# Graph attention on one core: edge steps of two slots and an accumulator that goes through TensorE and ScalarE

## The chip, the cores and the metric

One of the eight cores of a Trainium2 chip runs the whole program; the others are idle. The metric is device time in microseconds, from start to end of one execution. Engines are named as in the profile: PE is TensorE, DVE is VectorE, ACT is ScalarE, POOL is GpSimd, SP is SyncE, which here only issues DMAs.

## The reference

12,500 nodes with 256 features, 200,000 edges (src, dst), eight heads of 32. It is one attention layer over a graph with a residual and a layer norm:

```
q = (x @ Wq.T + bq) * 32**-0.5 ; k = x @ Wk.T + bk ; v = x @ Wv.T + bv    # per node, 8 heads
s = sum over a head of q[src] * k[dst]                                   # per edge and head
e = exp(s - max of s over the edges of the same src)
out = sum over the edges of e * v[dst] / sum of e                        # per src
y = layernorm(x + out @ Wo.T + bo)
```

## The kernel before

The program has three parts. `prepare` projects all nodes to q, k and v, writes a row [k | v and a one per head] of 520 floats per node to DRAM (`kv_rows`), sorts the edges by src, sorts the nodes by degree, and writes the q rows in that order (`q_perm`). `one_round` walks the edges; the diff touches only this part. `finish` divides, projects and normalises tile by tile.

A tile is 128 nodes of about the same degree, one per partition; there are 98 tiles. A tile's edges are walked in steps of G slots: in one step each partition handles G edges of its node. The number of steps of a tile is the largest degree in it, divided by G and rounded up. One round covers up to C edges of a node. STEPS is an upper bound that holds for any graph, fixed when the program is built: 598 before. The steps beyond the real ones work on a spare tile (number TILES) whose mask is NEG and whose columns are all 0, so all partitions gather row 0. A table `step_tab` holds tile and column of every step; each engine reads its entry into a register with `value_load`, which is a table load and some register operations on the engine's sequencer.

The accumulator `acc` lies in SBUF, VW = 264 columns per tile (eight heads of 32 sums and one weight sum). The softmax is computed online: `runmax` holds the maximum so far, and in each step the old accumulator is scaled by exp(old maximum − new maximum), which stands in `s` behind the G·8 scores.

All engines run their own loop over the same steps k, with B steps in a loop body, and meet on semaphores that count steps:

- GpSimd (`gather`, L931) issues G indirect DMAs per step, each 128 rows of 2080 bytes, into ring slot k mod U of `kv`. Before the last gather of a step it waits in `ready` (L923) for the indices, and for `pv_made` and `last_made` of the step that had the slot before.
- SyncE (`load_q`, L949 and L952) reads the tile number and loads q of the tile, into the ring `q`; it waits for `prod_made` of U steps ago.
- VectorE, in the order of `step`: sums of the products of k+1 (L797), weighting of the first V = G−1 slots of k (`weigh`, L825), look-up of step k+2 (L853, L854), copy of the old maximum (L802) and mask (L805) of k+1, new maximum of k+1 (L812), addition of the matmul sum of k−1 to the accumulator (`add_sum`, L844), product of k+2 (`score`, L790), scaling of the accumulator for k (`scale_acc`, L836), differences of k+1 (L818).
- ScalarE, per step: `indices` (L969 table load, L973) for the step U ahead, exp of k+1 (`weights`, L977), and the last slot's weighting, eight instructions of 33 columns, one per head (`weigh_last`, L987).
- TensorE (`total`, L1032 and L1034) multiplies an identity with the G weighted slots, so they add up in PSUM (`sum_ps`, two of them). A matmul of f32 shows as two records.

The waits on the semaphores are what sets the order between the engines; within an engine it is the order of the code.

## Time and profile before

| | us |
|---|---|
| median of 3 runs | 4026.59 |
| lowest, highest | 4025.29, 4100.18 |
| profiled execution | 4017.71 |
| its span in the profile | 4015.6 |
| VectorE busy | 3211.0 (80%) |
| GpSimd busy | 2447.6 (61%) |
| TensorE busy | 2227.2 (55%) |
| ScalarE busy | 1504.6 (37%) |

The share of a whole span mixes three stages. The edge loop is the stretch from about 1268 to 3723 us. Columns of the rows below are told with each view. "Idle before" of an engine is the time without work ahead of the instructions of a row, and what ended it; "issue" means that nothing which the profile shows was waited for. Sequencer work (waits, registers, branches, table loads) is not counted as busy; rows with a q behind the engine's name are of the sequencer. The clock PEclk is granted TensorE clock, 1 is full speed.

### The profile page before, as it was taken

To read this page: it belongs to the slowest core of one execution; us is meant where nothing else is said; L and a number is where in the kernel's file an instruction comes from. 1 tells how busy PE (TensorE), PEld (TensorE's weight loads), DVE (VectorE), ACT (ScalarE), POOL (GpSimd) and SP (SyncE) were. 2 spreads that over 40 slices of the span, in tenths; PEclk is the share of its full clock that TensorE was granted. 3 is DMA by queue.
4 is the path that set the end of the run, shared out by engine and by line. 5 is a ranking of instruction groups with operands and counts; after the bars stand their busy time and mean duration, and the time that the engine had idled before them with its cause. 6 is when DMAs were issued, how large, how long until landed. Compare 5 with 4: busy or idle time off the path is not lost. (4 is left out here: it accounts for less than half of the span.)

```text
span 4015.6 us, 59591 instructions
## 1 busy us (share of the span) xinstructions
PE 2227.2 (55%) x7109; PEld 1514.8 (38%) x7109; DVE 3211.0 (80%) x8164; ACT 1504.6 (37%) x6480; POOL 2447.6 (61%) x2365
## 2 busy tenths in 40 slices
PE   3999888653002555555555545555555555544776
PEld 3788775432001333333333333333333333323443
DVE  8554467799223999999999999999999999977776
ACT  0110002221001555555555555555555555534332
POOL 3221120003767777777777777777777777765677
PEclk9966568776555788778777787777877778766777
DMA  1211013226513788878887887888777788799222
GB/s 33 64 58 32 16 43 101 89 67 125 171 36 96 231 233 232 232 232 232 231 232 232 232 232 231 232 232 231 232 232 231 232 232 232 229 177 169 80 92 85
DMA packets 329217, 665.86 MB, mean 166 GB/s; under 512 B 63462, under 2 KB 191750, under 8 KB 329016
## 3 DMA queue, kind: packets, MB, share of 16 engines
q0 software_dynamic: 160768, 518.27, 46.4%
q1 hardware_dynamic: 168392, 146.96, 12.7%
q8 instruction: 20, 0.33, 0.0%
q14 instruction: 37, 0.30, 0.0%
HBM read 599.35 MB, written 65.86 MB: 166 GB/s over the span
## 5 line engine op out<-in xcount | busy, mean ns | idle before, releaser
L931 POOL DMA_INDIRECT kv<-kv_rows,idx x1794 | 1863.0, 1038 | 583.7 <-issue 538.5
L1032 PE MATMUL sum_ps<-pv,ident 128*128 128x264 f32 x2392 | 902.0, 512 | 1299.3 <-DVE pv L825 1299.3
L1032 PEld LDWEIGHTS sum_ps<-pv,ident 128*128 128x128 f32 x2392 | 511.3, 237 | 1712.1 <-DVE pv L825 1393.1
L987 ACT ACTIVATE pv<-kv,s 128x33 f32<-128x33 f32 x4784 | 1084.4, 309 | 53.9 <-ACT s L977 27.3
L790 DVE TENSOR_TENSOR prod<-kv,q 128x768 f32<-128x768 f32 x598 | 569.2, 952 | 59.7 <-DMA kv<-kv_rows,idx 59.6
L797 DVE TENSOR_REDUCE s<-prod 128x24 f32<-128x768 f32 x598 | 565.5, 946 | 0.0
L977 ACT ACTIVATE s<-s 128x32 f32<-128x32 f32 x598 | 137.0, 229 | 1126.1 <-DVE s L818 1126.1
L1034 PE MATMUL sum_ps<-pv,ident 128*128 128x264 f32 x1196 | 497.3, 508 | 0.0
L507 PE MATMUL hist_ps<-hot_lo,hot_hi 125*98 125x128 bf16 x1600 | 372.1, 409 | 121.7 <-DVE hot_hi L174 121.7
L825 DVE TENSOR_TENSOR pv<-kv,s 128x528 f32<-128x528 f32 x598 | 417.4, 698 | 0.3 <-ACT s L977 0.3
L507 PEld LDWEIGHTS hist_ps<-hot_lo,hot_hi 125*98 125x98 bf16 x1600 | 370.3, 259 | 123.2 <-issue 68.7
L492 POOL DMA_INDIRECT kv_st<-node_rows,node_id x98 | 102.8, 1049 | 464.4 <-issue 444.4
L472 POOL TENSOR_SCALAR hot_hi<-hi_b 125x320 bf16<-125x320 bf16 x140 | 149.7, 1072 | 377.8 <-PE hist_ps L507 356.7
L172 DVE TENSOR_SCALAR hot_lo<-lo_b 125x320 bf16<-125x320 bf16 x640 | 164.2, 334 | 206.5 <-PE hist_ps L507 206.5
L1034 PEld LDWEIGHTS sum_ps<-pv,ident 128*128 128x128 f32 x1196 | 296.6, 248 | 70.3 <-ACT pv L987 0.4
L844 DVE TENSOR_TENSOR acc<-acc,sum_ps 128x264 f32 x598 | 256.6, 429 | 22.2 <-PE sum_ps L1034 1.1
L575 ACT ACTIVATE kv_st<-kv_ps 128x256 f32<-128x256 f32 x98 | 37.6, 383 | 589.3 <-PE q_ps L519 589.3
L836 DVE TENSOR_TENSOR acc<-acc,s 128x264 f32 x598 | 255.0, 426 | 0.3
L518 PE MATMUL kv_ps<-w_sb,xt_sb 128*128 128x512 f32 x392 | 200.5, 636 | 0.0
L812 DVE TENSOR_REDUCE runmax<-s 128x32 f32 x598 | 123.7, 207 | 79.3
L973 ACT ACTIVATE idx<-cols 128x3 int32 x598 | 113.2, 189 | 139.0 <-DVE round_base L782 136.6
L1178 POOL DMA_INDIRECT x<-in_x_rows,node_id x98 | 112.7, 1150 | 56.9 <-issue 30.7
(164 smaller groups left out, 2450.5 us busy)
## 6 DMA issues: line engine op xcount, KB each, us to landing
q<-q_perm SPq DMA_DIRECT2D x598, 128.0 KB, 3.7
kv<-kv_rows,idx POOLq DMA_INDIRECT x1794, 4.0
kv_rows<-kv_st SPq DMA_DIRECT2D x98, 260.0 KB, 3.0
xt_sb<-in_xT SPq DMA_DIRECT2D x98, 128.0 KB, 3.2
node_rows<-q_st SPq DMA_DIRECT2D x98, 128.0 KB, 3.4
q_perm<-kv_st SPq DMA_DIRECT2D x98, 128.0 KB, 1.9
kv_st<-node_rows,node_id POOLq DMA_INDIRECT x98, 3.1
cols<-edge_keys,run_at POOLq DMA_INDIRECT x98, 2.5
```

The source lines that it names most:

```text
L172: dve.tensor_scalar(hot_lo[:, v, :], lo_b[:, c * CH:(c + 1) * CH], float(v), None, ALU.is_equal)
L507: last = pe.matmul(hist_ps[0:TILES, 0:P], hot_hi[:, :, e], hot_lo[:, :, e], start=c == 0 and e == 0, stop=c == CHUNKS - 1 and e == CH - 1)
L518: pe.matmul(ps[:, 0:b - a], xt_sb[:, j, kc, :], w_sb[:, kc, a:b], start=kc == 0, stop=False)
L790: dve.tensor_tensor(prod[:, :, :], kv[:, j, :, 0:D], q[:, j, :].unsqueeze(1).to_broadcast([P, G, D]), ALU.mult).then_inc(prod_made, 1)
L797: dve.tensor_reduce(s[:, b, 0:G * HEADS], prod[:, :, :].rearrange("p g (h d) -> p (g h) d", d=HD), AX.X, ALU.add).then_inc(scored, 1)
L825: dve.tensor_tensor(pv[:, b, 0:V * VW].rearrange("p (g h w) -> p g h w", g=V, w=HD + 1), kv[:, j, 0:V, D:KVW].rearrange("p g (h w) -> p g ...
L836: dve.tensor_tensor(at_tile, at_tile, s[:, b, G * HEADS:].unsqueeze(2).to_broadcast([P, HEADS, HD + 1]), ALU.mult).then_inc(acc_scaled, 1)
L844: dve.tensor_tensor(at_tile, at_tile, sum_ps[b][:, 0:VW], ALU.add).then_inc(acc_added, 1)
L931: pool.indirect_dma_start(out=kv[:, j, g, :], out_offset=None, in_=kv_rows, in_offset=bass.IndirectOffsetOnAxis(ap=idx[:, j, g:g + 1], axi ...
L987: last = act.activation(pv[:, b, V * VW + at_h:V * VW + at_h + HD + 1], kv[:, j, V, D + at_h:D + at_h + HD + 1], ACT.Copy, scale=s[:, b, V ...
L1032: pe.matmul(sum_ps[b][:, 0:VW], ident[:, :], pv[:, b, g * VW:(g + 1) * VW], start=g == 0, stop=False)
L1034: pe.matmul(sum_ps[b][:, 0:VW], ident[:, :], pv[:, b, V * VW:G * VW], start=False, stop=True).then_inc(summed, 1)
```

## The change

Steps have two slots (G = 2) and not three, a round has 40 columns per node and not 39, the rings have eight slots and not six, and loop bodies sixteen steps and not six. STEPS becomes 849. VectorE no longer reads and adds the matmul sum. Instead `carry` writes the scaled old accumulator into a third part of `pv`, TensorE adds it with a third matmul, and ScalarE copies the sum from PSUM to the accumulator (`store`), between the third and the fourth head of the next step; for that ScalarE reads the step's table entry a second time. `carry` of a step waits for the store of the step before. VectorE's look-up is cut in two: the table load right behind the sums of the products, the decoding behind the product. ScalarE makes its indices at the end of a step and not at the start. The scratch of the table building moves from `pv` to `kv`.

```diff
--- before.py
+++ after.py
@@ -36,14 +36,15 @@
 CHUNKS = EF // CH
 POOL_HOTS = 28
 CLIP = 1022
-G = 3
+G = 2
 QR = 2 * R
 BP = 65
-C = 39
+C = 40
 TAB = TILES + 1
-U = 6
+U = 8
 V = G - 1
-B = 6
+BEFORE_STORE = 3
+B = 16
 
 
 STEPS = C // G + (E // P + (TILES - 1) * (G - 1)) // G
@@ -695,11 +696,11 @@
         q = sb("q", [P, U, D])
         prod = sb("prod", [P, G, D])
         s = sb("s", [P, 2, (G + 1) * HEADS])
-        pv = sb("pv", [P, 2, G * VW])
...
@@ -797,9 +798,12 @@
                     dve.tensor_reduce(s[:, b, 0:G * HEADS], prod[:, :, :].rearrange("p g (h d) -> p (g h) d", d=HD),
                                       AX.X, ALU.add).then_inc(scored, 1)
 
-                def mask_scores(k, b, col, tile):
+                def old_maximum(k, b, tile):
 
                     dve.tensor_copy(s[:, b, G * HEADS:], runmax[:, bass.ds(tile * HEADS, HEADS)]).then_inc(old_copied, 1)
+
+                def mask_scores(k, b, col):
+
                     dve.wait_ge(scored, k + 1)
                     sv = s[:, b, 0:G * HEADS].rearrange("p (g h) -> p g h", h=HEADS)
                     dve.tensor_tensor(sv, sv, mflat[:, bass.ds(col, G)].unsqueeze(2).to_broadcast([P, G, HEADS]), ALU.add).then_inc(masked, 1)
@@ -827,58 +831,53 @@
                                       s[:, b, 0:V * HEADS].rearrange("p (g h) -> p g h", h=HEADS).unsqueeze(3).to_broadcast([P, V, HEADS, HD + 1]),
                                       ALU.mult).then_inc(pv_made, 1)
 
-                def scale_acc(k, b, tile, first=False):
-
+                def carry(k, b, tile, first=False):
                     if not first:
-                        dve.wait_ge(acc_added, k)
-                    dve.wait_ge(exp_made, k + 1)
-                    at_tile = acc[:, bass.ds(tile * VW, VW)].rearrange("p (h w) -> p h w", w=HD + 1)
-                    dve.tensor_tensor(at_tile, at_tile,
-                                      s[:, b, G * HEADS:].unsqueeze(2).to_broadcast([P, HEADS, HD + 1]), ALU.mult).then_inc(acc_scaled, 1)
-
-                def add_sum(k, b, tile):
-
-                    dve.wait_ge(acc_scaled, k + 1)
-                    dve.wait_ge(summed, k + 1)
-                    at_tile = acc[:, bass.ds(tile * VW, VW)]
-                    dve.tensor_tensor(at_tile, at_tile, sum_ps[b][:, 0:VW], ALU.add).then_inc(acc_added, 1)
+                        dve.wait_ge(acc_stored, k)
+                    dve.tensor_tensor(pv[:, b, G * VW:].rearrange("p (h w) -> p h w", w=HD + 1),
+                                      acc[:, bass.ds(tile * VW, VW)].rearrange("p (h w) -> p h w", w=HD + 1),
+                                      s[:, b, G * HEADS:].unsqueeze(2).to_broadcast([P, HEADS, HD + 1]), ALU.mult).then_inc(carry_made, 1)
 
                 dve.wait_ge(tab_ready, 1)
                 dve.wait_ge(runs_ready, 1)
 
-                tile_r = [dve.alloc_register(f"tile_{b}") for b in range(3)]
-                col_r = [dve.alloc_register(f"col_{b}") for b in range(3)]
-
-                def look_up(k, c):
-                    v = dve.value_load(step_tab[0:1, bass.ds(k, 1)], min_val=0, max_val=TAB * C * P - 1)
-                    dve.reg_mov(tile_r[c], v & (P - 1))
-                    dve.reg_mov(col_r[c], v >> PBITS)
+                tile_r = [dve.alloc_register(f"tile_{b}") for b in range(2)]
+                col_r = [dve.alloc_register(f"col_{b}") for b in range(2)]
+                entry_r = dve.alloc_register("entry")
+
+                def look_up(k):
+                    dve.reg_mov(entry_r, dve.value_load(step_tab[0:1, bass.ds(k, 1)], min_val=0, max_val=TAB * C * P - 1))
+
+                def decode(b):
+                    v = bounded(dve, entry_r, TAB * C * P - 1)
+                    dve.reg_mov(tile_r[b], v & (P - 1))
+                    dve.reg_mov(col_r[b], v >> PBITS)
 
                 def step(k, j, turn, peel=False, last=False):
 
                     b, b1 = j % 2, (j + 1) % 2
+                    tile, tile1, col1 = bounded(dve, tile_r[b], TILES), bounded(dve, tile_r[b1], TILES), bounded(dve, col_r[b1], TAB * C - G)
                     score_sum(k + 1, b1, peeled=peel and j == 0)
+                    look_up(k + 2)
+                    old_maximum(k + 1, b1, tile1)
                     weigh(k, j % U, b, peeled=peel and j < 2)
-
-                    tile, tile1, col1 = (bounded(dve, tile_r[j % 3], TILES), bounded(dve, tile_r[(j + 1) % 3], TILES),
-                                         bounded(dve, col_r[(j + 1) % 3], TAB * C - G))
-                    before = None if peel and j == 0 else bounded(dve, tile_r[(j + 2) % 3], TILES)
-                    look_up(k + 2, (j + 2) % 3)
-                    mask_scores(k + 1, b1, col1, tile1)
+                    mask_scores(k + 1, b1, col1)
+                    carry(k, b, tile, first=peel and j == 0)
                     maxima(k + 1, b1, tile1)
-                    if before is not None:
-                        add_sum(k - 1, b1, before)
                     if not last:
                         score(k + 2, (j + 2) % U, turn + (j + 2) // U)
-                    scale_acc(k, b, tile, first=peel and j == 0)
+                    decode(b)
                     differences(k + 1, b1, tile1)
 
-                look_up(0, 0)
-                look_up(1, 1)
+                look_up(0)
+                decode(0)
+                look_up(1)
+                decode(1)
                 score(0, 0, 0)
                 score_sum(0, 0, peeled=True)
                 tile, col = bounded(dve, tile_r[0], TILES), bounded(dve, col_r[0], TAB * C - G)
-                mask_scores(0, 0, col, tile)
+                old_maximum(0, 0, tile)
+                mask_scores(0, 0, col)
                 maxima(0, 0, tile)
                 score(1, 1, 0)
                 differences(0, 0, tile)
@@ -891,11 +890,8 @@
                     step(k, k - LOOPS * B, LOOPS * (B // U), last=k == STEPS - 2)
                 k = STEPS - 1
                 weigh(k, k % U, k % 2)
-                tile, before = bounded(dve, tile_r[k % 3], TILES), bounded(dve, tile_r[(k - 1) % 3], TILES)
-                add_sum(k - 1, (k - 1) % 2, before)
-                scale_acc(k, k % 2, tile)
-                add_sum(k, k % 2, tile)
-                for r in tile_r + col_r:
+                carry(k, k % 2, bounded(dve, tile_r[k % 2], TILES))
...
@@ -976,39 +972,54 @@
                     act.wait_ge(diffs_made, k + 1)
                     act.activation(s[:, b, :], s[:, b, :], ACT.Exp).then_inc(exp_made, 1)
 
-                def weigh_last(k, j, turn, b, peeled=False):
+                def weigh_heads(j, b, heads):
+
+                    for h in heads:
+                        at_h = h * (HD + 1)
+                        last = act.activation(pv[:, b, V * VW + at_h:V * VW + at_h + HD + 1], kv[:, j, V, D + at_h:D + at_h + HD + 1],
+                                              ACT.Copy, scale=s[:, b, V * HEADS + h:V * HEADS + h + 1])
+                    return last
+
+                def weigh_last(k, j, turn, b, stored=True, peeled=False):
 
                     act.wait_ge(exp_made, k + 1)
                     act.wait_ge(kv_in[j], 16 * G * turn + 16 * G)
                     if not peeled:
                         act.wait_ge(summed, k - 1)
-                    for h in range(HEADS):
-                        at_h = h * (HD + 1)
-                        last = act.activation(pv[:, b, V * VW + at_h:V * VW + at_h + HD + 1], kv[:, j, V, D + at_h:D + at_h + HD + 1],
-                                              ACT.Copy, scale=s[:, b, V * HEADS + h:V * HEADS + h + 1])
-                    last.then_inc(last_made, 1)
+                    weigh_heads(j, b, range(0, BEFORE_STORE))
+                    if stored:
+                        store(k - 1, 1 - b)
+                    weigh_heads(j, b, range(BEFORE_STORE, HEADS)).then_inc(last_made, 1)
+
+                def store(k, b):
+
+                    v = act.value_load(step_tab[0:1, bass.ds(k, 1)], min_val=0, max_val=TAB * C * P - 1)
+                    tile = bounded(act, v & (P - 1), TILES)
+                    act.wait_ge(summed, k + 1)
+                    act.activation(acc[:, bass.ds(tile * VW, VW)], sum_ps[b][:, 0:VW], ACT.Copy).then_inc(acc_stored, 1)
 
                 act.wait_ge(tab_ready, 1)
                 act.wait_ge(runs_ready, 1)
                 for j in range(U):
                     indices(j, j, 0)
                 weights(0, 0)
-                weigh_last(0, 0, 0, 0, peeled=True)
+                weigh_last(0, 0, 0, 0, stored=False, peeled=True)
                 for k in range(B):
-                    indices(k + U, k % U, 1)
                     weights(k + 1, (k + 1) % 2)
                     weigh_last(k + 1, (k + 1) % U, (k + 1) // U, (k + 1) % 2, peeled=k == 0)
+                    indices(k + U, k % U, 1)
                 with act.Fori(1, LOOPS - 1) as kk:
                     for j in range(B):
                         k = kk * B + j
-                        indices(k + U, j % U, kk * (B // U) + j // U + 1)
                         weights(k + 1, (j + 1) % 2)
                         weigh_last(k + 1, (j + 1) % U, kk * (B // U) + (j + 1) // U, (j + 1) % 2)
+                        indices(k + U, j % U, kk * (B // U) + j // U + 1)
                 for k in range((LOOPS - 1) * B, STEPS - 1):
+                    weights(k + 1, (k + 1) % 2)
+                    weigh_last(k + 1, (k + 1) % U, (k + 1) // U, (k + 1) % 2)
                     if k + U < STEPS:
                         indices(k + U, k % U, (k + U) // U)
-                    weights(k + 1, (k + 1) % 2)
-                    weigh_last(k + 1, (k + 1) % U, (k + 1) // U, (k + 1) % 2)
+                store(STEPS - 1, (STEPS - 1) % 2)
 
             @block.tensor
             def _(pe):
@@ -1023,19 +1034,17 @@
                     last = pe.matmul(tab_ps[2 * j + 1][:, 0:b - a], nsteps[0:TILES, :], past[0:TILES, a:b], start=True, stop=True)
                 last.then_inc(counts_made, 1)
 
-                def total(k, b, peeled=False):
+                def total(k, b):
 
                     pe.wait_ge(pv_made, k + 1)
-                    if not peeled:
-                        pe.wait_ge(acc_added, k - 1)
                     for g in range(V):
                         pe.matmul(sum_ps[b][:, 0:VW], ident[:, :], pv[:, b, g * VW:(g + 1) * VW], start=g == 0, stop=False)
                     pe.wait_ge(last_made, k + 1)
-                    pe.matmul(sum_ps[b][:, 0:VW], ident[:, :], pv[:, b, V * VW:G * VW], start=False, stop=True).then_inc(summed, 1)
-
-                for j in range(B):
-                    total(j, j % 2, peeled=j < 2)
-                with pe.Fori(1, LOOPS) as kk:
+                    pe.matmul(sum_ps[b][:, 0:VW], ident[:, :], pv[:, b, V * VW:G * VW], start=False, stop=False)
+                    pe.wait_ge(carry_made, k + 1)
+                    pe.matmul(sum_ps[b][:, 0:VW], ident[:, :], pv[:, b, G * VW:], start=False, stop=True).then_inc(summed, 1)
+
+                with pe.Fori(0, LOOPS) as kk:
                     for j in range(B):
                         total(kk * B + j, j % 2)
                 for k in range(LOOPS * B, STEPS):
```

## Rows read from the trace of the kernel before

**Rows 1.** source view of L790: count, duration ns min/median/max, first and last start

```profile
L790 DVE TENSOR_TENSOR prod<-kv,q x598: 949/951/992, 1267.8 to 3715.3; 128x768 f32<-128x768 f32 x200
```

**Rows 2.** groups of 1500 to 3300 us: busy, mean ns | idle before

```profile
L931 POOL DMA_INDIRECT kv<-kv_rows,idx x1347 | 1390.1, 1032 | 410.7 <-issue 410.7
L987 ACT ACTIVATE pv<-kv,s 128x33 f32<-128x33 f32 x3590 | 813.8, 309 | 41.1 <-ACT s L977 21.0 <-PE sum_ps L1034 4.4
...
L790 DVE TENSOR_TENSOR prod<-kv,q 128x768 f32<-128x768 f32 x449 | 427.1, 951 | 0.0
```

**Rows 3.** windows: stretch, us, busy per engine, PEclk, DMA share, GB/s

```profile
2000.00:2500.00 500.00, 264.68 (x750) 166.01 (x750) 467.94 (x1124) 266.17 (x1246) 385.99 (x375) 0.79 0.80 232
...
3557.00:3703.00 146.00, 71.19 (x164) 43.91 (x163) 104.01 (x244) 57.60 (x269) 91.10 (x82) 0.65 0.98 177
3760.00:3990.00 230.00, 169.43 (x566) 105.87 (x567) 183.93 (x730) 76.12 (x122) 179.11 (x162) 0.74 0.29 92
```

**Rows 4.** timeline, one step: start us, duration us, instruction

```profile
2508.26 0.95 DVE L797 TENSOR_REDUCE s<-prod 128x24 f32<-128x768 f32 x1
2508.38 0.23 ACT L977 ACTIVATE s<-s 128x32 f32<-128x32 f32 x1 [1.91 <-DVE s L818]
2508.79 1.82 ACT L987 ACTIVATE pv<-kv,s 128x33 f32<-128x33 f32 x8 [0.17 <-PE sum_ps L1034]
...
2509.13 0.70 DVE L825 TENSOR_TENSOR pv<-kv,s 128x528 f32<-128x528 f32 x1
...
2509.88 1.16 PE L1032 MATMUL sum_ps<-pv,ident 128*128 128x264 f32 x4 [1.12 <-DVE pv L825]
2509.89 0.17 DVE L802 COPY s<-runmax 128x8 f32 x1
2510.03 0.18 DVE L805 TENSOR_TENSOR s<-s,mask 128x24 f32<-128x24 f32 x1
2510.35 0.21 DVE L812 TENSOR_REDUCE runmax<-s 128x32 f32 x1
...
2510.57 0.43 DVE L844 TENSOR_TENSOR acc<-acc,sum_ps 128x264 f32 x1
...
2510.92 0.95 DVE L790 TENSOR_TENSOR prod<-kv,q 128x768 f32<-128x768 f32 x1
...
2511.79 0.43 DVE L836 TENSOR_TENSOR acc<-acc,s 128x264 f32 x1
2512.13 0.19 DVE L818 TENSOR_TENSOR s<-s,runmax 128x32 f32<-128x32 f32 x1
...
2512.35 0.23 ACT L977 ACTIVATE s<-s 128x32 f32<-128x32 f32 x1 [1.65 <-DVE s L818]
```

**Rows 5.** source view of L949, SyncE's first table load

```profile
L949 SPq TENSOR_LOAD <-tile_tab x598: 262/268/290, 1137.2 to 3683.6; - x200
```

**Rows 6.** timeline of ScalarE reading PSUM in the first part

```profile
149.54 0.38 ACT L575 ACTIVATE kv_st<-kv_ps 128x256 f32<-128x256 f32 x1
149.82 0.38 ACT L576 ACTIVATE kv_st<-kv_ps 128x256 f32<-128x256 f32 x1
```

**Rows 7.** source view of L969, ScalarE's table load

```profile
L969 ACTq TENSOR_LOAD <-step_tab x598: 272/278/303, 1259.8 to 3694.1; - x200
```

**Rows 8.** timeline, TensorE at the lower clock

```profile
2501.70 2.13 PE L1032 MATMUL sum_ps<-pv,ident 128*128 128x264 f32 x4 [2.29 <-DVE pv L825]
```

**Rows 9.** windows over rows 8 and over the step of rows 4

```profile
2499.20:2509.30 10.10, 6.22 (x13) 3.70 (x12) 9.43 (x23) 5.02 (x24) 7.66 (x9) 0.50 0.80 233
2509.60:2522.90 13.30, 5.88 (x23) 4.12 (x24) 12.40 (x33) 7.51 (x36) 10.25 (x11) 1.00 0.81 231
```

**Rows 10.** DMA queues from 3557 to 3703 us: packets, MB, share

```profile
q0 software_dynamic: 6714, 22.34, 87.2%
```

**Rows 11.** page, DMA queue that carries code: packets, MB, share

```profile
q8 instruction: 20, 0.33, 0.0%
```

**Rows 12.** page, DMA issues: count, us from issue to landing

```profile
kv<-kv_rows,idx POOLq DMA_INDIRECT x1794, 4.0
```

More of the change, by code:

```diff
@@ L697, in one_round @@
         s = sb("s", [P, 2, (G + 1) * HEADS])
-        pv = sb("pv", [P, 2, G * VW])
-        room = pv[:, :, :].rearrange("p b w -> p (b w)")
-        step_f, past, tile_f = room[:, 0:STEPS], room[:, STEPS:2 * STEPS], kv[0:1, U - 1, :, :].rearrange("p g w -> p (g w)")[:, 0:STEPS]
-        place_f = prod[0:1, :, :].rearrange("p g d -> p (g d)")[:, 0:STEPS]
+        pv = sb("pv", [P, 2, (G + 1) * VW])
+        room = kv[:, :, :, :].rearrange("p u g w -> p (u g w)")
+        step_f, past = room[:, 0:STEPS], room[:, STEPS:2 * STEPS]
+        tile_f, place_f = room[0:1, 2 * STEPS:3 * STEPS], room[0:1, 3 * STEPS:4 * STEPS]
         tab_ps = [pp("tab_ps0", [1, 512]), pp("tab_ps1", [1, 512]), pp("tab_ps2", [1, 512]), pp("tab_ps3", [1, 512])]
@@ L713, in one_round @@
             sem(x) for x in ("prod_made", "scored", "old_copied", "masked", "max_made", "diffs_made"))
-        exp_made, pv_made, last_made, acc_scaled, summed, acc_added = (
-            sem(x) for x in ("exp_made", "pv_made", "last_made", "acc_scaled", "summed", "acc_added"))
+        exp_made, pv_made, last_made, carry_made, summed, acc_stored = (
+            sem(x) for x in ("exp_made", "pv_made", "last_made", "carry_made", "summed", "acc_stored"))
         CUT = 512
@@ L893, in _ @@
                 weigh(k, k % U, k % 2)
-                tile, before = bounded(dve, tile_r[k % 3], TILES), bounded(dve, tile_r[(k - 1) % 3], TILES)
-                add_sum(k - 1, (k - 1) % 2, before)
-                scale_acc(k, k % 2, tile)
-                add_sum(k, k % 2, tile)
-                for r in tile_r + col_r:
+                carry(k, k % 2, bounded(dve, tile_r[k % 2], TILES))
+                for r in tile_r + col_r + [entry_r]:
                     dve.free_register(r)
```

## The prediction, made before the change was run

> **What bounds the kernel now.** I read the busy time by stage first, then the groups of the steady stretch, then one step in order of time, then the same step on TensorE at its two clocks, and last the stretch at the end of the edge loop.
>
> The edge loop runs from the first product at 1267.8 us to the last at 3715.3 us, 598 steps [rows 1]. That is 2447.5 of the 4015.6 us span; only this part changes. In the steady part a step takes 1800/449 = 4.01 us: VectorE starts 449 products in 1800 us and none of them waits for data [rows 2]. VectorE is busy for 468 of 500 us [rows 3], and its nine instructions follow one another with hardly a gap [rows 4]. So VectorE sets the step.
>
> Second in line is GpSimd. It starts a gather every (1390.1+410.7)/1347 = 1.337 us [rows 2], three a step, which is also 4.01 us: no room above VectorE. This number becomes the floor when VectorE gets shorter. TensorE and ScalarE have slack inside a step today, because nothing that they make is needed at once: the sum of step k is added one step later.
>
> The last idle steps are another regime. Between 3557 and 3703 us there are 82/3 = 27.3 steps, so 5.34 us each, with the DMA engines at 0.98 of their time [rows 3]. These are the steps beyond the real work: all partitions gather the same row.
>
> **How many steps.** The nodes are sorted by degree and a tile needs ceil(largest degree / G) steps. From the reference's inputs (98 tiles, largest degrees 32 down to 7) that is 559 real steps of 598 with three slots, and 813 of 849 with two. Check on the trace: 559 × 4.01 + 39 × 5.34 = 2450 us, against 2447.5. After the change 813 steps are to be paid with a shorter step, and 36 idle ones. Gathers fall from 1794 to 1698. To break even, (2450 − 133)/813 = 2.85 us a step is allowed (the 133 is the idle part, below).
>
> **VectorE's step after.** By row: the product of 768 columns takes 0.95, the 264 column ones 0.43, so 1.03 ns a column [rows 4]. From start to start: sum of products 0.87 − 256 × 1.03 ns = 0.60; copy of the old maximum about 0.12; weighting of one slot 0.34 (as L836 to L818); mask 0.15; carry 0.34; maximum 0.2 (as L812 to L844); product 0.87 − 0.26 = 0.61; difference 0.10. Sum 2.46 us. The addition of 0.35 is gone (L844 to L790), and the wait between mask and maximum (L805 to L812, 0.32) is filled by the carry. The look-up is sequencer work of under a microsecond; its halves lie behind the 0.60 and the 0.61 and cost 0 to 0.1, I take 0. The loop's end comes 51 times and not 98; a gain of at most a few tens of us if VectorE set the step, which it won't; I take 0. Alone, VectorE would allow 813 × 2.46 = 2000 us.
>
> **GpSimd's step after.** 2 × 1.337 = 2.67 us. It has now less than before to wait for, and a ring of eight buffers. SyncE loads q 849 times instead of 598; it waits on a product eight steps back, so only its traffic counts: 2 gathers and one q in about 2.8 us is no more per us than 3 gathers and one q in 4.01. The larger table is built well before the loop: SyncE reads its first entry at 1137.2 us, 130 us before the first product [rows 5]. Both cost nothing.
>
> **What the accumulator's new way costs.** This is the step on which the forecast rests. ScalarE now does, per step: exp, three heads, the store of the previous sum, five heads, indices. The heads are handed on 0.216 us apart ((1.82 − 0.31)/7, [rows 2, 4]). The store reads PSUM like L575: 0.38 long, and the next one starts 0.28 after it [rows 6]. ScalarE alone: 0.41 to the first head + 3 × 0.216 + 0.28 + 5 × 0.216 + 0.10 + exp to exp 0.1 = 2.6 us. That is no bound by itself. But the accumulator makes two rings that close once per step.
>
> Ring 1, through VectorE. The store of k sits between the heads of k+1; carry(k+1) waits for it, and behind carry on VectorE are queued the maximum, the product and the difference of k+2, for which the next exp waits. From the start of exp to the start of the store: 0.41 from exp to the first head [rows 4] and three heads give 1.05; beside them the new table read, 0.28 [rows 7] and the register operations around it, may end sooner or later: 0.9 to 1.2 for the whole. Then the store 0.38, carry 0.34, maximum 0.2, product 0.61, difference 0.19, and three hand-overs of 0.03. Sum 2.7 to 3.0, I take 2.80.
>
> Ring 2, through TensorE. After the store come five heads (0.28 + 4 × 0.216 + 0.31 = 1.45), then TensorE's last slot and the carry, one behind the other, then the next store. Two such matmuls from a standing start, four records, take 1.16 us at full clock and 2.13 us at half clock [rows 4, 8]; 0.05 + 0.04 for the hand-overs (L825 ends 2509.83, TensorE starts 2509.88, [rows 4]). Sum 2.70 at full clock, 3.67 at half clock. carry_made is earlier than last_made and is not late; the late one is always last_made.
>
> Today the half clock costs nothing: six records, 1.5 times the 2.13, are about 3.1 of 4.01 us and nobody waits. After the change its price is on the path. The granted clock has two levels, 1.2 and 2.4 GHz: one stretch stands at 0.50 and the next at 1.00 [rows 9]. Its mean is 0.79 in the loop, so full for 0.58 of the time, 0.65 in the idle steps, and 0.74 in the stage after the loop [rows 3]. Its share after the change is not shown; bounds are 0.30 full (the idle steps) and 1 (the stretch at 1.00). After the change TensorE is busy about as in the last stage, so I take 0.53, between 0.48 there and 0.58 now. Steps per us: 0.53/2.80 + 0.47/3.67 = 0.317, so 3.15 us a step.
>
> **The sum.** Real steps 813 × 3.15 = 2561. Idle steps: of 5.34 us the gathers' queue has 0.872 [rows 10], 4.66 or 1.55 a gather, the rest 0.6; two gathers give 3.7, times 36 is 133. Together 2694 against 2450: +244. The profiled execution has 4017.7 us, 2 us of them outside its span; that makes 4262. The median shown is 4026.6, 9 us higher; I say 4265.
>
> **Rivals.**
>
> A, faster. The rings close sooner and GpSimd sets the step: 813 × 2.67 + 133 = 2304, −146, 3870. For it: the ScalarE work is 2.6, both rings at full clock begin at 2.70, and a TensorE that is at full clock nearly always would leave the step at GpSimd's pace. It decides below 2.75 us a step, which is 2% faster. Against it: every one of three terms must fall at its low end. Chance 0.21.
>
> B, the rings hold but TensorE keeps the full clock: 813 × 2.80 + 133 = 2409, −41, 3977. For it: at full clock six records take about 1.7 us (1.5 times 1.16), now of 4.01 and then of 2.8. Against it: in the last stage TensorE is busy 169/230 = 74% of the time and in the loop 53%, and yet the mean clock is lower there [rows 3]. The Trainium skill (TensorE: Matmul & The Clock Gate, Part 1: The HAM clock gate) says that the default is the throttled clock and that being busy releases it; by that rule the change raises the share of full clock and the time would be this one. The trace agrees only from the idle steps to the loop (0.65 to 0.79), not on to the last stage. Chance 0.17, up to 2.95 us a step.
>
> C, slower still: the longer loop body costs a code load in each of the 51 passes. In the trace there are 20 code transfers of 0.33 MB in all on the one queue [rows 11], fewer than the 98 passes, so today the loop runs without them. What one would cost is not shown: nothing at the least, and at the most what a transfer from HBM takes from issue to landing, 4.0 us for a gather [rows 12]. With 3 us it is +150, 4415. The Trainium skill (Runtime: NRT & Kernel Launch, Instruction fetch mechanics) says that code is held in two blocks of 256 instructions and that a jump back to a block that is no longer there stalls; by my count of the listing (about 25 VectorE instructions a step) sixteen steps are some 400 instructions, which may lie in three blocks, where six steps were about 155. The trace before can't show it. Chance 0.11.
>
> D: the change does nothing measurable in this loop, 4027. It would need the step to fall by exactly the rise in steps; chance 0.02, taken with B.
>
> **How the numbers follow.** Forecast 0.49: its own range comes from the share of full clock, 0.75 (2.98 us, 4120) to 0.45 (3.22 us, 4320). The range 3870 to 4400 reaches from A to just under C; what is left out is about half of A and most of C with the end of the forecast's own. 2% of 4027 is 81 us, about what a measurement can tell from no change. Faster 0.21 (A), within 2% 0.18 (B, D and a little of the forecast), slower 0.61.
>
> **What would show it.** Right: in the steady part VectorE waits before the carry for the store (ScalarE) in most steps, ScalarE waits before the store for TensorE's sum where the granted clock is 0.50 and hardly where it is 1.00; step lengths in two kinds, near 2.8 and near 3.7; GpSimd now waits for last_made. Idle steps of 3.7. Wrong: VectorE waiting at the product for gathers and GpSimd without a gap, which is A; a granted clock near 1 throughout, which is B; one long gap per sixteen steps on VectorE or ScalarE together with some fifty code transfers, which is C. VectorE's own instructions adding up to much more than 2.46 would break the working at its first term.

## The result and the profile after

The changed kernel takes 4292.2 us (median of 4, 4290.1 to 4296.2) against 4035.7 us of the kernel before in the same runs: ratio 1.065, 95% interval 1.061 to 1.068. One of the four runs of the kernel before, 4100.2 us, was in a slower state of the chip and is left out of the ratio. The forecast was 4265 us, in a range of 3870 to 4400. The profiled execution has a span of 4289.5 us, 274 more than before. All but 2 us of it is in the edge loop. First the source view of the product (duration min/median/max, first and last start), then the windows of the steady part and of the idle steps (busy time per engine, granted clock, DMA share, GB/s):

```profile
L791 DVE TENSOR_TENSOR prod<-kv,q x849: 672/681/755, 1269.4 to 3989.0; 128x512 f32<-128x512 f32 x170
```

```profile
1500.00:3500.00 2000.00, 1272.88 (x3760) 689.99 (x3758) 1553.37 (x5011) 1572.67 (x6890) 1279.35 (x1253) 0.90 0.75 209
3870.00:3980.00 110.00, 68.19 (x176) 36.23 (x175) 73.28 (x234) 72.80 (x321) 61.49 (x58) 0.77 0.92 176
```

The loop has 849 products in 2719.6 us, where it had 598 in 2447.5 [rows 1]: +272. VectorE's share fell from 94% to 78% of a steady stretch [rows 3], GpSimd's from 77% to 64%, ScalarE's rose from 53% to 79%. No engine is full any more; what sets the step is a ring of waits: a chain that starts at one instruction and comes back to the same instruction one step later. The granted clock rose from 0.79 to 0.90.

The steps are of three kinds: the plain step, the one with a code load (place 1), and those at half clock behind it. From start to start of the product, by place in the pass of 16 steps (medians over the 813 real steps, us; a pass is one run through the loop body):

```
place   0     1     2     3     4 to 8   9     10 to 13   14    15
       2.85  5.97  3.79  3.83   2.86    3.04     2.86    3.00  2.78
```

The plain step, in order of time (start, duration; TensorE at full clock):

```profile
2019.72 0.39 ACT L999 ACTIVATE acc<-sum_ps 128x264 f32 x1
...
2020.01 1.16 ACT L979 ACTIVATE pv<-kv,s 128x33 f32<-128x33 f32 x5
...
2020.26 0.43 DVE L837 TENSOR_TENSOR pv<-acc,s 128x264 f32<-128x264 f32 x1 [0.22 <-ACT acc L999]
...
2020.70 0.68 DVE L791 TENSOR_TENSOR prod<-kv,q 128x512 f32<-128x512 f32 x1
...
2021.22 0.71 PE L1043 MATMUL sum_ps<-pv,ident 128*128 128x264 f32 x2 [0.49 <-ACT pv L979]
2021.30 0.18 DVE L822 TENSOR_TENSOR s<-s,runmax 128x24 f32<-128x24 f32 x1
...
2021.51 0.22 ACT L973 ACTIVATE s<-s 128x24 f32<-128x24 f32 x1 [0.25 <-DVE s L822]
...
2021.77 0.75 ACT L979 ACTIVATE pv<-kv,s 128x33 f32<-128x33 f32 x3
2021.77 0.61 PE L1045 MATMUL sum_ps<-pv,ident 128*128 128x264 f32 x2
...
2022.58 0.39 ACT L999 ACTIVATE acc<-sum_ps 128x264 f32 x1
```

Both rings can be walked here. Store 2019.72 to 2020.11, carry 2020.26 (VectorE idle for 0.22 before it, ended by the store), maximum, product, difference until 2021.48, exp, three heads, store 2022.58: ring 1. Five heads until 2021.17, last slot 2021.22, carry behind it until 2022.38, store 2022.58: ring 2. 2.86 us from store to store.

One step in sixteen and those behind it (same columns):

```profile
2187.36 0.69 DVE L798 TENSOR_REDUCE s<-prod 128x16 f32<-128x512 f32 x1 [3.02 <-ACT pv L979]
...
2188.91 1.25 PE L1041 MATMUL sum_ps<-pv,ident 128*128 128x264 f32 x2 [3.66 <-DVE pv L829]
...
2192.11 0.39 ACT L999 ACTIVATE acc<-sum_ps 128x264 f32 x1 [0.82 <-PE sum_ps L1045]
...
2192.66 0.43 DVE L837 TENSOR_TENSOR pv<-acc,s 128x264 f32<-128x264 f32 x1 [1.14 <-ACT acc L999]
...
2193.62 1.25 PE L1043 MATMUL sum_ps<-pv,ident 128*128 128x264 f32 x2 [0.82 <-ACT pv L979]
...
2194.66 1.09 PE L1045 MATMUL sum_ps<-pv,ident 128*128 128x264 f32 x2
...
2195.94 0.39 ACT L999 ACTIVATE acc<-sum_ps 128x264 f32 x1 [1.04 <-PE sum_ps L1045]
```

The sum of products at 2187.36 comes after 3.02 us of idle VectorE. The view puts this down to ScalarE's heads, but the wait in front of the sum is for the heads of three steps earlier, which had ended some 6 us before. It is VectorE's sequencer that stands: it jumps back to the start of the body at 2183.84 and shows nothing until 2187.05 (L886). ScalarE's sequencer stands as well, from its jump at 2186.54 to 2190.04 (L1011); that is hidden behind VectorE's delay, because the difference for which ScalarE's next exp waits ends only at 2190.08.

TensorE has nothing to do for 3.66 us in this time, and from 2188.91 on it runs at half clock. In the second step behind the load its last slot and carry take from 2193.62 to 2195.75, 2.13 us, and the store at 2195.94 waits 1.04 us for them; the carry at 2192.66 had waited 1.14 us for its store, which had itself waited for TensorE. Such a step is 3.8 us. On the page one queue shows what the 3 us are (packets, MB; first the kernel before, then the changed one):

```profile
q14 instruction: 37, 0.30, 0.0%
```

```profile
q14 instruction: 547, 4.48, 0.3%
```

The row that I had put forward, [rows 11], was the other code queue, which has hardly changed (21 transfers). 510 more of 8 KB in 51 passes is ten a pass. The waits of 1500 to 3500 us (total, times, longest) in short: the carry waits for the store in 548 of 627 steps, the store for TensorE's sum in 83. The sum of products stands 35 times but up to 3.6 us; these are the code loads, under ScalarE's name.

```profile
DVE pv L837 <- ACT acc L999: 197.9, 548, 1.2
DVE s L798 <- ACT pv L979: 112.4, 35, 3.6
ACT acc L999 <- PE sum_ps L1045: 77.5, 83, 1.0
```

The account of the 813 real steps, from the means by place (50.8 passes): 813 × 2.856 = 2322 us of plain steps; the code load 3.02 × 50.8 = 153; the steps at half clock behind it 2.04 × 50.8 = 104; the other places that are longer or shorter than the plain step 13. Sum 2592, or 3.19 a step.

### The profile page after: what moved, and what is told of

The parts are those of the page before. It is cut to its first block and busy times, and to the rows that moved or that the text cites. A ratio compares the mean times of both kernels' runs of the same rounds, so it can differ in the third digit from the quotient of the medians.

```text
span 4289.5 us, 77637 instructions
## 1 busy us (share of the span) xinstructions
PE 2663.5 (62%) x8615; PEld 1641.2 (38%) x8615; DVE 3069.9 (72%) x9574; ACT 2358.0 (55%) x9839; POOL 2330.8 (54%) x2269
## 5 line engine op out<-in xcount | busy, mean ns | idle before, releaser
L979 ACT ACTIVATE pv<-kv,s 128x33 f32<-128x33 f32 x6792 | 1621.4, 312 | 48.5 <-ACT s L973 25.8
L1041 PE MATMUL sum_ps<-pv,ident 128*128 128x264 f32 x1698 | 676.5, 484 | 701.8 <-DVE pv L829 701.8
L1043 PE MATMUL sum_ps<-pv,ident 128*128 128x264 f32 x1698 | 660.5, 474 | 423.7 <-ACT pv L979 423.3
L798 DVE TENSOR_REDUCE s<-prod 128x16 f32<-128x512 f32 x849 | 582.2, 686 | 177.1 <-ACT pv L979 141.6
L791 DVE TENSOR_TENSOR prod<-kv,q 128x512 f32<-128x512 f32 x849 | 579.1, 682 | 21.7 <-DMA kv<-kv_rows,idx 21.5
L1045 PE MATMUL sum_ps<-pv,ident 128*128 128x264 f32 x1698 | 575.3, 424 | 0.0
L837 DVE TENSOR_TENSOR pv<-acc,s 128x264 f32<-128x264 f32 x849 | 367.2, 433 | 276.9 <-ACT acc L999 270.4
L999 ACT ACTIVATE acc<-sum_ps 128x264 f32 x849 | 331.2, 390 | 149.4 <-PE sum_ps L1045 107.7
L973 ACT ACTIVATE s<-s 128x24 f32<-128x24 f32 x849 | 189.0, 223 | 400.1 <-DVE s L822 400.1
L829 DVE TENSOR_TENSOR pv<-kv,s 128x264 f32<-128x264 f32 x849 | 367.7, 433 | 1.2 <-ACT s L973 0.3
L803 DVE COPY s<-runmax 128x8 f32 x849 | 149.8, 176 | 144.8 <-issue 142.4
L969 ACT ACTIVATE idx<-cols 128x2 int32 x849 | 161.7, 191 | 139.8 <-DVE round_base L783 136.5
```

The costliest lines, as they stand in the source:

```text
L791: dve.tensor_tensor(prod[:, :, :], kv[:, j, :, 0:D], q[:, j, :].unsqueeze(1).to_broadcast([P, G, D]), ALU.mult).then_inc(prod_made, 1)
L798: dve.tensor_reduce(s[:, b, 0:G * HEADS], prod[:, :, :].rearrange("p g (h d) -> p (g h) d", d=HD), AX.X, ALU.add).then_inc(scored, 1)
L829: dve.tensor_tensor(pv[:, b, 0:V * VW].rearrange("p (g h w) -> p g h w", g=V, w=HD + 1), kv[:, j, 0:V, D:KVW].rearrange("p g (h w) -> p g ...
L837: dve.tensor_tensor(pv[:, b, G * VW:].rearrange("p (h w) -> p h w", w=HD + 1), acc[:, bass.ds(tile * VW, VW)].rearrange("p (h w) -> p h w" ...
L973: act.activation(s[:, b, :], s[:, b, :], ACT.Exp).then_inc(exp_made, 1)
L979: last = act.activation(pv[:, b, V * VW + at_h:V * VW + at_h + HD + 1], kv[:, j, V, D + at_h:D + at_h + HD + 1], ACT.Copy, scale=s[:, b, V ...
```

## The experiments

Ratios are to the kernel before, timed beside each run; "before" is 4017 to 4042 us in these. Theory 1: two rings, and a code load in each pass that also costs TensorE its clock. The steps by place are read from each run's starts of the product.

**Shorter body.**

```diff
-B = 16
+B = 8
```

> The changed kernel with loop bodies of 8 steps instead of 16; nothing else. Theory 1 (two separate causes: a code load of about 3.1 us on VectorE and ScalarE in each pass of the 16-step loop, and behind it, because TensorE stood idle, some three steps at half clock of 3.8 instead of 2.86 us): with 187 VectorE instructions a pass no code is loaded, the clock stays full, a step is 2.87 us, the loop 813 x 2.87 + 36 x 3.64 = 2464 us, the whole 4035 us, about the kernel before. Rival H (the half clock comes by itself, as it did before the change, and the code loads only add to it): the loads go (-158) but one step in six stays at 3.8 us: 4130 us. Rival N (the long step in each pass is the loop's own end, not code): no fewer long steps per step, rather more: 4290 us or above.

Measured: 4061.5 us, ratio 1.009 (1.006 to 1.012), 231 less than the change as it stands. Code transfers and the window from 1500 to 3400 us:

```profile
q14 instruction: 41, 0.34, 0.0%
```

```profile
1500.00:3400.00 1900.00, 1219.89 (x3914) 635.49 (x3912) 1618.14 (x5219) 1639.26 (x7175) 1494.98 (x1305) 1.00 0.79 228
```

The transfers are gone and the granted clock is 1.00 throughout: the half clock did not come by itself, it followed the stall. H and N fall. The plain step stays at 2.86; two steps of every eight, right behind the jump, take 3.04 and 3.12. For them above all, the real steps took 37 us more than expected; the idle steps took 9 less.

**TensorE's order, in the 16-step body.**

```diff
-                    pe.wait_ge(last_made, k + 1)
-                    pe.matmul(sum_ps[b][:, 0:VW], ident[:, :], pv[:, b, V * VW:G * VW], start=False, stop=False)
                     pe.wait_ge(carry_made, k + 1)
-                    pe.matmul(sum_ps[b][:, 0:VW], ident[:, :], pv[:, b, G * VW:], start=False, stop=True).then_inc(summed, 1)
+                    pe.matmul(sum_ps[b][:, 0:VW], ident[:, :], pv[:, b, G * VW:], start=False, stop=False)
+                    pe.wait_ge(last_made, k + 1)
+                    pe.matmul(sum_ps[b][:, 0:VW], ident[:, :], pv[:, b, V * VW:G * VW], start=False, stop=True).then_inc(summed, 1)
```

> The changed kernel, with 16-step bodies, but TensorE takes the carry before the last slot: behind last_made there is then one matmul and not two. Theory 1 (ring 2 through TensorE sets the steps at half clock and only those; ring 1 through VectorE sets the others): steps at half clock fall from 3.8 to about 2.9 us, steps at full clock stay at 2.86, code loads stay: 51 x 2.9 x 0.9 = 133 us less, 4160 us. Rival (the steps of 3.8 us are ScalarE or VectorE catching up after the code load): no change, 4290. Rival (ring 2 sets the full-clock steps too): these shorten as well, by up to 0.4 us, below 4050.

Measured: 4199.1 us, ratio 1.042 (1.037 to 1.047), 93 less. Places 3 and 4 of the pass fall from 3.52 and 3.24 (means) to 2.95 and 2.88. The step right behind the load (place 2) keeps its 3.79 us:

```profile
2159.80 1.25 PE L1041 MATMUL sum_ps<-pv,ident 128*128 128x264 f32 x2 [4.65 <-DVE pv L829]
...
2160.20 0.69 DVE L791 TENSOR_TENSOR prod<-kv,q 128x512 f32<-128x512 f32 x1
...
2161.72 1.09 PE L1045 MATMUL sum_ps<-pv,ident 128*128 128x264 f32 x2
...
2163.01 0.39 ACT L999 ACTIVATE acc<-sum_ps 128x264 f32 x1 [0.84 <-PE sum_ps L1045]
...
2163.99 0.68 DVE L791 TENSOR_TENSOR prod<-kv,q 128x512 f32<-128x512 f32 x1
```

Here all that TensorE needs has been made, and its six records run back to back, 3.01 us at half clock; their order can't matter. So ring 2 sets the later steps at half clock and TensorE's whole work the first one. The gain is made up otherwise than I expected: of 83 us in the real steps, places 2 to 6 give 58, and 28 come from steps at full clock, of which some (places 0 and 10 to 13) fall from 2.86 to 2.77. To that small part the second rival was right; why those places and no others is open.

**Carry behind the product, and both together,** in the 8-step body:

```diff
-                    carry(k, b, tile, first=peel and j == 0)
                     maxima(k + 1, b1, tile1)
                     if not last:
                         score(k + 2, (j + 2) % U, turn + (j + 2) // U)
+                    carry(k, b, tile, first=peel and j == 0)
                     decode(b)
```

Both versions also make the copy of the old maximum wait for the carry of two steps before, which reads the same part of `s`. "Both" has TensorE's new order as well.

> The changed kernel with 8-step bodies and the carry behind the next product on VectorE instead of ahead of the maximum. Theory 1 (ring 1, store - carry - maximum - product - difference - exp - heads - store, sets the 2.86 us): 0.8 us leave this ring, the next bound is ring 2 at full clock or GpSimd, 2.70 us: 813 x 2.72 + 131, 3920 us. Rival (ScalarE's own work and its second table load set 2.86): no change against 8-step bodies alone, 4035. Rival (the carry is now late for TensorE): 0.3 us more a step, 4250.

> 8-step bodies, carry behind the product, and TensorE takes the carry before the last slot. Theory 1: both rings are below GpSimd's two gathers (2.67 us a step), which then sets the step: 813 x 2.68 + 131, 3885 us, and VectorE waits at the product for gathers. Rival (ScalarE, 2.6 us of work and the hand-overs, is the bound): 2.75 to 2.8 us a step, 3960. Rival (carry ahead of the last slot makes TensorE wait for the late carry): slower than the version with the carry late alone.

Measured: late alone 4066.8 us, 1.011 (1.008 to 1.013), as with B = 8 alone; both 4103.3 us, 1.018 (1.013 to 1.023). Theory 1 missed both times. In the second TensorE waits 1.1 us for the late carry in every step, its last slot queued behind it (total us, times, longest, 1500 to 3400 us):

```profile
PEld sum_ps L1045 <- DVE pv L839: 697.4, 640, 1.2
```

which is the rival that both texts named. That late alone gains nothing fits the next three runs: ring 2 was still closed. It was not tested further.

**One ring at a time, without touching VectorE's order.** b8_swap is B = 8 with TensorE's new order; b8_early is B = 8 with ScalarE's table load ahead of the exp:

```diff
+                        tile = tile_of(k)
                         weights(k + 1, (j + 1) % 2)
-                        weigh_last(k + 1, (j + 1) % U, kk * (B // U) + (j + 1) // U, (j + 1) % 2)
+                        weigh_last(k + 1, (j + 1) % U, kk * (B // U) + (j + 1) // U, (j + 1) % 2, tile)
```

This is the part in the loop's body; `tile_of` is the table load that `store` had in it.

> 8-step bodies (step 2.86 us at full clock, whole 4061 us) and TensorE takes the carry before the last slot; VectorE and ScalarE in the order of the changed kernel. Theory 1 (at full clock ring 1 through VectorE sets the step, ring 2 through TensorE only at half clock): almost nothing, since the clock is full throughout: 4040 to 4061. Rival (ring 2 sets the step at full clock): 0.15 to 0.2 us a step less, 3920.

> 8-step bodies and ScalarE's table load for the store moved ahead of the exp, so that the store can follow the third head at once; orders of all engines otherwise as in the changed kernel. Theory 1 (ring 1 from store over carry, maximum, product, difference, exp, three heads, and the store waits 0.18 us for its table load): 0.15 us a step less, until ring 2 or GpSimd at 2.70: 813 x 0.15 = 120 us less, 3940 us. Rival (VectorE's own sequence and its waits set 2.86, as the version with the late carry suggests): no change, 4061. Rival (the load now delays the exp): slower, 4150.

> 8-step bodies, ScalarE's table load ahead of the exp, and TensorE takes the carry before the last slot. Theory 1: ring 1 is 0.15 us shorter and ring 2 is well below it, GpSimd's two gathers or ring 1 set 2.68 to 2.72 us: 3925 us. Rival (VectorE's own sequence): as with 8-step bodies alone, 4061.

Measured: 4051.4 us, 1.003 (0.999 to 1.007); 4029.0 us, 0.997 (0.992 to 1.001); together 3912.2 us, 0.968 (0.960 to 0.976). Opening ring 2 leaves the plain step at 2.85, opening ring 1 at 2.86, opening both gives 2.72. So at full clock the rings are equally long; my 2.70 for ring 2 was short. In b8_early it can be read off, now that no table load delays the store:

```profile
2502.17 1.16 ACT L979 ACTIVATE pv<-kv,s 128x33 f32<-128x33 f32 x5
...
2503.38 0.71 PE L1049 MATMUL sum_ps<-pv,ident 128*128 128x264 f32 x2 [0.51 <-ACT pv L979]
...
2503.93 0.61 PE L1051 MATMUL sum_ps<-pv,ident 128*128 128x264 f32 x2
...
2504.74 0.39 ACT L1002 ACTIVATE acc<-sum_ps 128x264 f32 x1
```

Heads end 2503.33, TensorE starts 2503.38 and ends 2504.54, the store starts 2504.74. The hand-over to ScalarE costs 0.20 us and not 0.04; with it ring 2 is 2.86 at full and 3.83 at half clock, which are the steps measured. (The 32 us of b8_early against b8 are not the ring's: the two steps behind the jump fell to 2.86 and 2.97.)

In the version with both, ring 1 sets the step, shorter now by the table load:

```profile
2499.85 0.37 ACT L1002 ACTIVATE acc<-sum_ps 128x264 f32 x1
...
2500.37 0.43 DVE L837 TENSOR_TENSOR pv<-acc,s 128x264 f32<-128x264 f32 x1
...
2501.41 0.17 DVE L822 TENSOR_TENSOR s<-s,runmax 128x24 f32<-128x24 f32 x1
...
2501.62 0.22 ACT L973 ACTIVATE s<-s 128x24 f32<-128x24 f32 x1 [0.24 <-DVE s L822]
...
2501.88 0.75 ACT L979 ACTIVATE pv<-kv,s 128x33 f32<-128x33 f32 x3
...
2502.53 0.37 ACT L1002 ACTIVATE acc<-sum_ps 128x264 f32 x1
```

From store to store 2.68 us (2.73 in the mean of 1500 to 3400 us); the carry starts 0.15 behind the end of the store, as it does in all the versions with the carry in its first place, and the store 0.65 behind the first head, where b8_early has 0.81. One might take GpSimd for the bound instead, since it stands only for the 0.30 us between two gathers. These are the groups of 1500 to 3400 us, the last line from b8:

```profile
L927 POOL DMA_INDIRECT kv<-kv_rows,idx x1391 | 1475.8, 1061 | 424.0 <-issue 340.2 <-ACT idx L969 82.9 <-ACT pv L979 0.9
...
L791 DVE TENSOR_TENSOR prod<-kv,q 128x512 f32<-128x512 f32 x696 | 473.5, 680 | 0.0
```

```profile
L927 POOL DMA_INDIRECT kv<-kv_rows,idx x1305 | 1495.8, 1146 | 405.0 <-issue 399.0 <-DVE pv L829 2.1 <-ACT idx L969 2.1
```

(1475.8 + 424.0)/1391 = 1.366 us a gather, 2.73 a step. But in b8, where the rings set the step, the same sum gives 1.457 and 2.91, again the step: a gather stretches with VectorE's step (see the end). And no product waits for its data. So GpSimd is not shown to be the bound in any of the two-slot versions; of the two that this run's text names, it is ring 1. This version is 3% faster than the kernel before and 9% faster than the change.

**The parts alone.** First the sizes without the new accumulator, then the new accumulator without the sizes:

The comments tell which version a line belongs to; in g2_old and g2_old6 the table's scratch moves to `kv` too.

```diff
-G = 3          # kernel before
+G = 2          # g2_old and g2_old6
-C = 39
+C = 40
-U = 6
+U = 8          # g2_old alone
-B = 6
+B = 8          # g2_old alone
```

```diff
-G = 2          # changed kernel
+G = 3          # g3_new
-C = 40
+C = 39
-U = 8
+U = 6
-B = 16
+B = 6
```

> The kernel before with only the sizes of the change: two slots, 40 columns, rings of 8, bodies of 8 steps (and the table's scratch in kv, which the longer table needs). VectorE still adds the sum, still scales in place, and looks up in one part behind the weighting. Theory 1 (VectorE sets the step and its look-up of 1.2 us from the exp on is no longer covered by a weighting of 0.43 us): 3.5 to 3.7 us a step, 813 x 3.6 + 131, 4700 us; so the new accumulator and the split look-up do pay, against this. Rival (the look-up is covered by something else): 2.46 + 0.35, 2.85 us a step, 4030.

> The kernel before with two slots and 40 columns alone; rings and bodies stay at 6 (the run with bodies of 8 mixed up tile registers at each loop end, because three register sets rotate, so part of its sums went to other tiles). Theory 1: as that run, 3.69 us a step, 4700 us. Rival (the register mix-up made it slow): 4050 us.

Measured: 4697.7 us, 1.163 (1.154 to 1.172), and 4711.0 us in a single run. Both are within 11 us of what was expected. g2_old adds part of its sums to other tiles, so its result is wrong; g2_old6 does not, and takes as long. VectorE stands 0.62 us before the copy of the old maximum in every step, behind its own look-up, and TensorE is at half clock throughout (g2_old6: waits; then the window of 1500 to 3400 us):

```profile
DVE s L802 <- issue: 316.8, 510, 0.7
```

```profile
1500.00:3400.00 1900.00, 1248.60 (x2042) 511.17 (x2041) 1484.44 (x4594) 1086.61 (x5101) 1095.07 (x1020) 0.50 0.64 178
```

> The changed kernel with three slots, 39 columns, rings and bodies of 6: the new accumulator and look-up alone. Theory 1 (VectorE falls to about 3.3 us, ring 2 is 2.86 at full clock and 3.8 at half, GpSimd's three gathers take 3.9 to 4.0): GpSimd sets the step, 3.95 us, 559 x 3.95 + 208, 3985 us; within 2% of before. Rival (GpSimd was slowed by waiting for VectorE alone and the rings are what counts): 3.3 to 3.5 us a step, 3700 us.

Measured: 4277.5 us, 1.065 (1.063 to 1.066). Both theories missed it. GpSimd does set the step, but its gathers got longer (groups; waits; then the timeline):

```profile
L927 POOL DMA_INDIRECT kv<-kv_rows,idx x1276 | 1512.0, 1185 | 389.0 <-issue 314.0 <-ACT idx L969 75.0
```

```profile
DVE prod L791 <- DMA kv<-kv_rows,idx: 448.7, 389, 2.0
```

```profile
2500.23 0.71 DVE L829 TENSOR_TENSOR pv<-kv,s 128x528 f32<-128x528 f32 x1
2500.41 1.40 POOL L927 DMA_INDIRECT kv<-kv_rows,idx  x1 [0.30 <-issue]
...
2502.96 0.96 DVE L791 TENSOR_TENSOR prod<-kv,q 128x768 f32<-128x768 f32 x1 [1.44 <-DMA kv<-kv_rows,idx]
2503.42 1.38 POOL L927 DMA_INDIRECT kv<-kv_rows,idx  x1 [0.30 <-issue]
```

(1512.0 + 389.0)/1276 = 1.49 us a gather against 1.337 [rows 2], 4.47 a step. VectorE now waits at the product. The long gathers end 0.87 and 0.88 us after the end of a VectorE instruction with two inputs in SBUF: 2501.81 after 2500.94, 2504.80 after 2503.92.

**Longer bodies in the kernel before.** B = 18 and B = 12 for B = 6:

> The kernel before with bodies of 18 steps and not 6, so about 460 VectorE and 318 ScalarE instructions a pass. Theory 1 (a pass over some 256 to 512 instructions reloads code at its end, whatever the kernel): code transfers appear, about ten for each of the 32 passes, VectorE stands 3 to 4.4 us in each: +100 to +140 us, 4150. Rival (the loads cost only because the new kernel's rings have no slack): transfers appear, but under 20 us.

> The kernel before with bodies of 12 steps: about 308 VectorE and 212 ScalarE instructions a pass. Theory 1a (what counts is more than 256 instructions): loads on VectorE in each of 48 passes, +150 us, 4180. Theory 1b (what counts is whether the body lies within two blocks of 256, by where it starts): none or few, 4020, some us less than before for the fewer loop ends.

Measured: 4111.1 us, 1.023 (1.021 to 1.025), and 4268.8 us, 1.063 (1.060 to 1.065). Code transfers, B = 18 first:

```profile
q14 instruction: 202, 1.65, 0.1%
```

```profile
q14 instruction: 280, 2.29, 0.2%
```

In both one step of the pass is long: 6.8 us with B = 18, 9.7 us with B = 12, against 3.97. So 2.8 us times 32 passes, and 5.7 times 48. The loads belong to the length of a body and not to the new rings; but 306 VectorE instructions cost twice what 457 did, with five transfers a pass each time. The long step shows why, B = 18 first:

```profile
2261.07 0.95 DVE L797 TENSOR_REDUCE s<-prod 128x24 f32<-128x768 f32 x1 [2.90 <-ACT pv L987]
2261.93 0.70 DVE L825 TENSOR_TENSOR pv<-kv,s 128x528 f32<-128x528 f32 x1
```

```profile
2230.89 0.95 DVE L797 TENSOR_REDUCE s<-prod 128x24 f32<-128x768 f32 x1 [3.05 <-ACT pv L987]
2233.99 0.71 DVE L825 TENSOR_TENSOR pv<-kv,s 128x528 f32<-128x528 f32 x1 [2.15 <-issue]
```

With B = 12 VectorE stands twice, behind the jump and again one instruction later. Where the body starts in its block was not varied, so what makes the second stop is open. ScalarE loads nothing in either: its sequencer goes on 0.2 us after each of its jumps, with 204 and 302 instructions a pass. In the changed kernel it has 374 and stands like VectorE, which would account for ten transfers a pass and not five.

## Why the prediction came out right, and where it did not

The direction and the two rings were right. That the total was met so closely (+272 us of loop, forecast as +244) is in part luck, since two large terms were off in opposite ways: 2561 us forecast for the real steps, 181 less for the half clock, 153 more for the code loads, 46 more for the plain step (2.856 and not 2.80) and 13 for the rest make the 2592 measured.

- Number of steps and idle steps: right. The idle steps took 3.64 us each (forecast 3.7).
- Ring 1, 2.80: measured 2.85, with ring 2 opened. From ScalarE's store to the carry it takes 0.15 us and not 0.03.
- Ring 2, 2.70 and 3.67: measured 2.86 and 3.8. The term that was too small is the hand-over from TensorE to ScalarE, 0.20 and not 0.04. It explains both values.
- The share of full clock, taken as 0.53: this step failed. The mean clock of 0.90 means 0.80 at full, and without code loads it is 1.00. The half clock was to cost 285 us and cost 104. I had taken the share from the last stage's rows [rows 3], a stage with other work. What the runs show in its place: TensorE is at full clock in the steady part of this loop unless a stall has left it idle; the code loads did so once a pass, for 3.3 us and more. So rival B was right on the clock. The rule of the Trainium skill (TensorE: Matmul & The Clock Gate, Part 1: The HAM clock gate), that being busy releases the throttle, agrees with b8 (64% busy, clock 1.00); g2_old6 (66% busy, clock 0.50) shows that the busy share alone does not tell which clock is granted.
- The code load, kept out of the sum as rival C with 3 us a pass: it happens, 3.0 us a pass, 153 us, and it is the cause of the half clock that is left. Both the price and the sign to know it by were in the prediction, and it was kept out of the sum as unlikely (0.11). Rival C itself, 4415, was not met, since it left the half clock at its forecast price. The rule of the Trainium skill (Runtime: NRT & Kernel Launch, Instruction fetch mechanics: a jump back to a block no longer held stalls) fits: 155 and 189 VectorE instructions a pass load nothing, 306, 374 and 457 do; on ScalarE 302 load nothing and 374 do (records of the trace from jump to jump).
- VectorE alone, 2.46: low by about 0.1. The table load is not covered by the sum of products (the copy starts 0.85 after it, not 0.60), but mask and maximum hand on after 0.09 each and not 0.15 and 0.20. The fastest steps of b8_late are 2.60. VectorE alone was on no path here.
- Rival A, GpSimd's 2.67 as a floor: not seen. The 1.337 us a gather of [rows 2] is no floor either: it has gathers in it that VectorE stretched; undisturbed, two take 2.60. Opening both rings led to 2.68 to 2.83 us a step, set by ring 1.

That two slots alone make the kernel slower is shown by the 4698 and 4711 us; with the same sizes the new accumulator, the split look-up and the later indices together (b8, 4061.5) take 636 us less than g2_old. Which of them pays was not tested. Not shown is why the late carry makes steps alternate between 2.6 or 2.7 and 3.2 us.

## What to carry to other kernels

When work moves to engines with slack, walk each ring that it closes (who waits for it, what is queued behind the waiting instruction, until the same instruction again) and sum it at both TensorE clocks; rings of equal length must be opened together, one alone shows nothing. An engine with no gap between its instructions need not be the bound: look for who waits for its results. Count the instructions of a loop body on every engine before making it longer: the load behind a jump costs its own time and then TensorE's clock. Read every code queue of the page, not one. Where a wait is put down to an engine that had long been done, look at the sequencer of the waiting engine.

## What the runs showed of the hardware

- The busy share of TensorE alone does not tell its clock: it is 66% busy at 0.50 throughout in g2_old6 (two matmuls in 3.7 us) and 64% busy at 1.00 throughout in b8 (three in 2.9 us). The lower clock itself makes the share high, since the same work fills twice the time.
- TensorE to ScalarE takes 0.20 us behind the modelled end of a matmul (in no version with a store is it under 0.19), TensorE to VectorE 0.11 (3722.75 to 3722.86 us at the end of the loop before), ScalarE's store to VectorE 0.15.
- An indirect gather on GpSimd takes 1.0 us alone and up to 1.79 us (g3_new) when it meets a VectorE instruction with two SBUF inputs; it then ends 0.87 us after that instruction. In g3_new all 568 gathers of 1500 to 3300 us that took over 1.04 us end 0.87 to 0.88 us after a product, a weighting or a carry. The Trainium skill (SBUF — State Buffer, SBUF: two separate sides) tells of a port pair that the two engines lock against each other; the fixed distance agrees.
